# Counting edges on one core of a graph kernel: packed window register, one eviction per window, and both counting stretches of a block in a row

## The chip, the core and the metric

One core of one Trainium2 chip runs the whole kernel in one launch. The metric is device time in microseconds (us), the median of a few runs. A profiled execution gives the span of the program on the core and everything that the rows below show. TensorE is called PE, VectorE DVE, ScalarE ACT, GpSimd POOL and SyncE SP, as in the profile; PEld is PE's loading of weights, and a q behind a name (ACTq) is the engine's sequencer.

## What is computed

Four graph layers in a residual stack over 1250 nodes of 512 features and 20000 edges; the edges are sorted by `dst`. Two layers hold two convolutions each, so there are six:

```python
h = relu(layernorm(x)); x = x + relu(mean_in(h) @ W_l.T + b_l + h @ W_r.T)              # L0
h = relu(layernorm(x)); x = x + sage(relu(sage(h)))                                     # L1A, L1B
h = relu(layernorm(x)); x = x + layernorm(h + relu(h @ W_self.T + b + mean_out(h @ W_neigh.T + b_n)))  # L2
h = relu(layernorm(x)); x = x + gcn(relu(gcn(h)))                                       # L3A, L3B
```

`mean_in` and the sums in `sage` and `gcn` gather the rows of the sources of a node's edges (`segment_sum(x[src], dst)`), `mean_out` those of its targets.

## The kernel before

**Tiling.** The nodes are padded to 1280, ten tiles of 128 (`NT`). All six convolutions work with one dense matrix of edge counts between nodes: `count16` (targets on partitions) and its transpose `countT16`, integers of 16 bits. A sum over neighbours is then 20 matmuls of 128 x 512 per tile of nodes (`aggregate`, L1217), with the counts staged as floats by ACT (`stage`, L480, two buffers `cstage`) and the features as a high and a low part (`p_hi`, `p_lo`).

**Counting.** The matrix is built at the start of the program by one-hot matmuls. A block is one tile of 128 targets, a window is 64 of them, so a block has windows h = 0 and 1 and there are 20 windows. The sorted edges lie in tiles of 128. A table says for every window at which edge tile it begins and how many it touches, in groups of `RING` = 6 tiles. For this graph the windows take 6, 3, then eight times 2, then ten times 1 groups, 35 in all: blocks 1 to 4 have two groups in each window, blocks 5 to 9 one. For one group of six tiles DVE writes six one-hots of the source (`src_hot`, 128 x 640, `givers`, L717) and three of the receiver (`dst_hot`, L715), ACT the other three receivers (`receivers`: three Abs into `apart`, L446, and one Relu over all three, L450), and PE makes 12 matmuls of 320 columns (`count`, L1112). There is one ring of six slots, so DVE and ACT are at most one group ahead of PE. The sign of the receiver's number says to which half of 640 the source belongs, so a window's sums stand in PSUM as 64 targets of the lower half on partitions 0 to 63 and of the upper half on 64 to 127. ACT takes them out with two activations of 64 partitions x 640 (`counts_of`, L428), each with an accumulated sum for the degrees, and puts them straight into `count16` by target. SP transposes each block of `count16` by DMA (L288).

**Registers.** PE, DVE and ACT loop over the groups of a window with bounds from the table (L240, L1123). ACT and DVE load 12 registers for two blocks at a time at the top of their loops (6 at some ends), three for each window; PE loads two for a block.

**Order.** The counting is interleaved by hand with the dense work of the first convolution, L0: PE turns the features of block b (`turn`, L1133) and makes the two products of block b - 1, 12 matmuls of 512 columns each (`first_p`, `first_q`, L1140). In the loop PE does: count (b, 0), p of b - 1, count (b, 1), turn b, q of b - 1. ACT does: deviation of b, receivers (b, 0), eviction (b - 1, 1), receivers (b, 1), phi of b - 1, eviction (b, 0), hi of b. So an eviction stands behind the receivers of the window that follows. DVE does: givers (b, 0), own of b - 2, features of b, givers (b, 1), `p_lo` of b - 1, statistics of b + 1, lo of b. Each engine works strictly in its order; semaphores tie them: a matmul of a group waits for `first_rows` (the Relu of ACT) and `givers_ready` (DVE), a hot waits for `hot_used` (PE), the eviction for `counts_ready` (the last matmul of the window, L1118), `turn` for `z_ready` (DVE).

**After the counting** the six convolutions run one behind another, and PE has nearly no idle time in them.

## Time and profile before

| | us |
|---|---|
| median of 3 runs (722.85 to 723.21) | 723.08 |
| the profiled execution | 723.23 |
| its span | 721.5 |
| PE busy, whole span | 671.5 (93%) |
| DVE busy | 408.4 (57%) |
| ACT busy | 286.8 (40%) |

The chain of work that ended last goes by 81% over PE, 5% over issue, 5% DVE and 3% ACT. The engines' busy times overlap, so they don't add up to the span. PE is "busy" too when it runs at half its clock, which some stretches show.

### The profile page before, as it was taken

The page shows a single profiled execution, that of the slowest core. Times are in us where ns is not written, and L with a number is a line of the kernel's source. Part 1 is how long each engine was busy: PE and PEld are TensorE (multiplying, and loading weights), DVE is VectorE, ACT ScalarE, POOL GpSimd, SP SyncE. Part 2 cuts the span into 40 slices and gives each one's busy share as a digit, 9 for nine tenths or more (in the row PEclk, how much of TensorE's full clock was granted, in tenths as well). Part 3 has the DMA queues.
Part 4 walks back from the last instruction along what each step waited for, and adds up shares of the span by engine and source line. Part 5 has one row for each costly group of instructions (what it writes and reads, how often), then busy time and mean ns, then how long its engine had stood idle before and what let it go on. Part 6 is the DMA issues. An engine that isn't in the chain of part 4 may idle for free.

```text
span 721.5 us, 11380 instructions
## 1 busy us (share of the span) xinstructions
PE 671.5 (93%) x3199; PEld 526.2 (73%) x3200; DVE 408.4 (57%) x951; ACT 286.8 (40%) x525; POOL 18.3 (3%) x26
## 2 busy tenths in 40 slices
PE   4948888889899999999999999999999899999997
PEld 3325565666688888888888888888877678887786
DVE  6977776666357544332443466655799871247333
ACT  2656565576343222465212342212444352223321
POOL 2000000000000000000000000000322000000000
PEclk9979999999899999999999999999999999999999
DMA  7101211011402000210000210000200000000011
GB/s 248 48 1 25 72 31 22 18 36 36 106 0 73 1 0 0 76 58 1 0 0 0 75 58 1 0 0 1 75 0 1 0 2 1 0 1 0 31 59 55
DMA packets 22801, 21.94 MB, mean 30 GB/s; under 512 B 13676, under 2 KB 13988, under 8 KB 22760
## 3 DMA queue, kind: packets, MB, share of 16 engines
q1 hardware_dynamic: 21480, 18.85, 9.2%
q10 hardware_dynamic: 1280, 2.56, 1.0%
q8 instruction: 24, 0.39, 0.2%
q14 instruction: 17, 0.14, 0.1%
HBM read 15.57 MB, written 2.56 MB: 25 GB/s over the span
## 4 chain that ended last, share of the span: by engine, by line
PE 81%; issue 5%; DVE 5%; ACT 3%; ACTq 2%; DVEq 2%; DMA 1%; SPq 0%
PE ps L1217 35%; PE ps L1140 33%; PE ps L1112 8%; PE ps L1133 3%; ACTq L240 1%; DMA wstage<-in_L_gnn_W_l 1%; DVEq L240 1%; ACT cstage L480 1%; PE ps L1092 1%; DVE src_hot L717 1%; ACT count L428 1%; DVE own L948 1%; ACT apart L446 1%; PE ps L1080 0%; DVE stats L695 0%
## 5 line engine op out<-in xcount | busy, mean ns | idle before, releaser
L1217 PE MATMUL ps<-p_hi,cstage 128*128 128x512 f32 x600 | 236.2, 394 | 6.4 <-issue 4.6
L1217 PE MATMUL ps<-p_lo,cstage 128*128 128x512 f32 x600 | 235.0, 392 | 0.0
L1140 PE MATMUL ps<-w_hi,hT_hi 128*128 128x512 f32 x400 | 162.4, 406 | 2.1 <-DVE hT_lo L756 2.0
L1140 PE MATMUL ps<-w_hi,hT_lo 128*128 128x512 f32 x400 | 156.6, 391 | 0.0
L1140 PE MATMUL ps<-w_lo,hT_hi 128*128 128x512 f32 x400 | 156.0, 390 | 0.0
L1217 PEld LDWEIGHTS ps<-p_hi,cstage 128*128 128x128 f32 x600 | 113.6, 189 | 31.9 <-issue 8.4
L1217 PEld LDWEIGHTS ps<-p_lo,cstage 128*128 128x128 f32 x600 | 113.6, 189 | 23.3
L920 DVE SCALAR_TENSOR_TENSOR own<-ps,nodal,own 128x512 f32 (+1 forms) x60 | 44.9, 749 | 124.6 <-PE ps L1217 124.2
L480 ACT CAST cstage<-countT 128x1280 fp32r (+1 forms) x50 | 62.6, 1262 | 90.9 <-PE ps L1217 90.0
L1112 PE MATMUL ps<-src_hot,dst_hot 128*128 128x320 bf16 x420 | 76.2, 330 | 22.0 <-ACT dst_hot L450 14.4
L717 DVE TENSOR_SCALAR src_hot<-iota,nodeT 128x640 bf16<-128x640 f16 x210 | 74.5, 381 | 25.5 <-PE ps L1112 13.1
L1140 PEld LDWEIGHTS ps<-w_hi,hT_hi 128*128 128x128 f32 x400 | 75.3, 188 | 18.6 <-DVE hT_lo L756 1.8
L1140 PEld LDWEIGHTS ps<-w_hi,hT_lo 128*128 128x128 f32 x400 | 75.1, 188 | 16.7
L1140 PEld LDWEIGHTS ps<-w_lo,hT_hi 128*128 128x128 f32 x400 | 75.3, 188 | 13.9
L1112 PEld LDWEIGHTS ps<-src_hot,dst_hot 128*128 128x128 bf16 x420 | 38.6, 106 | 54.0 <-DVE src_hot L717 22.7
L467 ACT ACTIVATE hT_hi<-ps 128x512 fp32r<-128x512 f32 x60 | 35.7, 596 | 78.7 <-PE ps L1133 78.5
L763 DVE TENSOR_TENSOR p_lo<-ps,p_hi 128x512 f32 (+1 forms) x40 | 27.6, 691 | 64.2 <-ACT p_hi L473 64.0
L473 ACT ACTIVATE p_hi<-ps 128x512 f32 (+1 forms) x40 | 23.9, 598 | 77.5 <-PE ps L1140 77.4
L756 DVE SCALAR_TENSOR_TENSOR hT_lo<-ps,hT_hi 128x512 fp32r<-128x512 f32 x60 | 41.0, 684 | 5.7 <-ACT hT_hi L467 5.2
L437 ACT ACTIVATE nodal<-mv,eps (+1 forms) x40 | 11.8, 295 | 79.6 <-DVE mv L704 67.1
L1133 PE MATMUL ps<-ident,z 128*128 128x128 f32 x240 | 36.8, 276 | 4.6 <-DVE z L743 4.3
L1133 PEld LDWEIGHTS ps<-ident,z 128*128 128x128 f32 x240 | 28.9, 141 | 12.4 <-issue 5.4
(130 smaller groups left out, 477.8 us busy)
## 6 DMA issues: line engine op xcount, KB each, us to landing
x<-in_x ACTq DMA_DIRECT2D x1, 2304.0 KB
out_x<-x SPq DMA_DIRECT2D x9, 256.0 KB
wstage<-in_L_gnn_W SPq DMA_DIRECT2D x2, 1024.0 KB, 5.2
wstage<-in_L_gnn_W_l SPq DMA_DIRECT2D x1, 1024.0 KB, 8.8
w_own<-in_L_gnn_W_r SPq DMA_DIRECT2D x1, 1024.0 KB, 9.4
vec<-in_L_gnn_b SPq DMA_DIRECT2D x4, 256.0 KB, 5.5
wstage<-in_L_gnn_W1l SPq DMA_DIRECT2D x1, 1024.0 KB, 5.6
wstage<-in_L_gnn_W1r SPq DMA_DIRECT2D x1, 1024.0 KB, 5.4
```

The lines of the kernel that those rows point to most:

```text
L240: _, found = nc.values_load_multi_w_load_instructions(for_hots[0:1, bass.ds(2 * b, 2 * blocks), 0:3], engines=[engine.engine], bass_reorde ...
L467: nc.scalar.activation(hT_hi[:, r, :, :], ps[:, HT + r, :].rearrange("p (k n) -> p k n", k=KF), ACT.Relu).then_inc(hi_done, 1)
L473: nc.scalar.activation(p_hi[:, bass.ds(i, 1), :], ps[:, p_bank(s, r), :], ACT.Copy, scale=1.0 if CONVS[s]["own"] else dis[:, bass.ds(i, 1) ...
L480: nc.scalar.copy(cstage[:, r, :, :], columns(s, i)).then_inc(stage_ready, 1)
L717: nc.vector.tensor_scalar(src_hot[:, e, :], iota[:, :], nodeT[:, 1, bass.ds(t + e, 1)], None, ALU.is_equal).then_inc(givers_ready, 1)
L756: nc.vector.scalar_tensor_tensor(hT_lo[:, r, :, :], ps[:, HT + r, :].rearrange("p (k n) -> p k n", k=KF), 0.0, hT_hi[:, r, :, :].bitcast(F ...
L763: nc.vector.tensor_tensor(p_lo[:, bass.ds(i, 1), :], ps[:, p_bank(s, r), :], p_hi[:, bass.ds(i, 1), :].bitcast(F32), ALU.subtract).then_in ...
L920: nc.vector.scalar_tensor_tensor(own_, ps[:, AGG + r:AGG + r + 1, :], scale[:, bass.ds(i, 1)], own_, ALU.mult, ALU.add).then_inc(t_done, 1)
L1112: last = nc.tensor.matmul(ps[:, COUNT + 2 * h + k, 0:NS // 2], dst_hot[:, e, :], src_hot[:, e, k * (NS // 2):(k + 1) * (NS // 2)], start=F ...
L1133: last = nc.tensor.transpose(ps[:, HT + r, k * P:(k + 1) * P], z[:, r, k * P:(k + 1) * P], ident[:, :])
L1140: last = nc.tensor.matmul(ps[:, bank, :], a[:, r, k, :], w[:, slot, k, :], start=n == 0, stop=n == len(pairs) - 1)
L1217: last = nc.tensor.matmul(ps[:, AGG + r, :], cstage[:, part, k, :], p_[:, k, :], start=n == 1, stop=n == 2 * len(parts) * NT)
```

## The change

One register of the table per window holds both the first edge tile and the number of tiles (first tile in the low 8 bits). Every engine loads it once per window and keeps its own count of visited tiles. Eviction is one activation of 128 partitions x 640: `count16` now holds, for block b, the two source halves on the partitions and the two windows side by side. The transposing DMAs go by window, 20 instead of 10, and write a `countT16` in which the staging copies read 64 counts, then the other window's 64. For L2, which needs `count16` by target, two quarters are swapped through DRAM (`swap`) by four DMAs in SP's queue. ACT makes four of six receivers. PE does both counting stretches of a block, with the turning between them, and then both products. The steps of the table, the order of the first weights (W_l in two halves ahead of x) and the first two blocks are written anew.

```diff
-    HALF = RING // 2
+    BY_ACT = 4
-    def visits_of(engine, b, blocks):
-        _, found = nc.values_load_multi_w_load_instructions(
-            for_hots[0:1, bass.ds(2 * b, 2 * blocks), 0:3], engines=[engine.engine], bass_reorder=False)
...
+    def visits_of(engine, visited, b, h):
+        _, (packed,) = nc.values_load_multi_w_load_instructions(
+            tiles_of[0:1, window(b, h)], engines=[engine.engine], bass_reorder=False)
+        t0, length = engine.snap(packed & 255), engine.snap(packed >> 8)
+        n0 = engine.snap(visited, min_val=0, max_val=NW * (ETP + RING))
+        offset = engine.snap(t0 - n0)
...
+        engine.reg_mov(visited, n1)
+        return n0, n1, offset
 # SP
-            order = [("f", 0), ("v", rows[0]), ("f", 1), ("v", rows[1]), ("t", 0), ("t", 1), loads[0]]
+            order = [("f", 0), ("f", 1), ("f", 2), ("v", rows[0]), ("v", rows[1]), ("t", 0), ("t", 1), loads[0]]
...
+                    for h in range(2):
+                        sp.wait_ge(counts_out, 2 * what + h + 3)
+                        sp.dma_start_transpose(
+                            countT16[:, 2 * what + h, :, :].rearrange("p (c q) d -> p c (q d)", q=2),
+                            count16[:, what, h * NS:(h + 1) * NS]).then_inc(cT_loaded, 16)
 # ACT
-            act.wait_ge(src_loaded, 32 + 16 * bool(REST))
+            for k, loaded in enumerate((dst_loaded, src_loaded)):
+                act.wait_ge(loaded, 16 * (2 + bool(REST)))
+                nc.scalar.copy(e_f[:, k, :, :], e_int[:, k, :, :]).then_inc(cast_done, 1)
+            act.wait_ge(first_loaded[1], 16)
             act.wait_ge(x_pad_set, 1)
             dma_rows(act, x_dram, x, x_loaded)
...
-                for q in range(2):
-                    nc.scalar.activation(
-                        count16[WIN * h:WIN * h + WIN, bass.ds(b, 1), q * NS:(q + 1) * NS].rearrange(
-                            "p o (a n) -> p (o a) n", a=2),
...
+                nc.scalar.activation(count16[:, bass.ds(b, 1), h * NS:(h + 1) * NS].rearrange("p o (a n) -> p (o a) n", a=2),
+                                     ps[:, COUNT + 2 * h:COUNT + 2 * h + 2, 0:NS // 2], ACT.Copy,
+                                     accum_out=deg_win[:, bass.ds(b, 1), h]).then_inc(counts_out, 1)
...
+                deviation(0, b)
+                receivers(b, 0)
+                counts_of(b, 0)
+                receivers(b, 1)
+                hi(L0, b, r)
+                counts_of(b, 1)
+                phi(L0, b - 1, 1 - r)
 # DVE
+                givers(b, 0)
                 features(L0, b, r)
-                givers(b, 1, *second)
+                first_own(b - 2)
+                givers(b, 1)
+                lo(L0, b, r)
+                if not (isinstance(b, int) and b == NT - 1):
+                    statistics(0, b + 1)
                 p_rest(L0, b - 1, 1 - r)
 # PE
-                n1 = visits_end(b)
-                count(b, 0, n1[0])
+                count(b, 0)
+                turn(L0, b, r)
+                count(b, 1)
                 first_p(b - 1, 1 - r)
-                count(b, 1, n1[1])
-                turn(L0, b, r)
                 first_q(b - 1, 1 - r)
...
+            count(0, 0)
+            turn_first(1, (0, 1))
+            count(0, 1)
+            turn_first(1, (2, 3))
+            count(1, 0)
             pe.wait_ge(wlo_done, 2 * KF)
             turn(L0, 0, 0)
-            with pe.Fori(1, NT - 1, 2) as b0:
+            count(1, 1)
+            first_p(0, 0)
+            turn(L0, 1, 1)
+            first_q(0, 0)
+            with pe.Fori(2, NT - 1, 2) as b0:
```

ACT between the two windows of a block, in the loop, before: `apart` and `dst_hot` are the receivers (L442 to L450 their loop), `count_49` the eviction, here of the window (b - 1, 1), with the receivers of (b, 1) behind it.

```order
L450 ACTIVATE dst_hot<-apart 128x384 [waits hot_used]
L442 REGISTER_ALU
L442 COMPARE_AND_BRANCH
L426 REGISTER_ALU
L428 ISA [waits counts_ready]
L428 ACTIVATE count_49,deg_parts<-ps 64x640
L428 ISA
L428 ACTIVATE count_49,deg_parts<-ps 64x640
L442 UNCONDITIONAL_BRANCH
L442 ISA
L446 ISA [waits first_rows]
L446 ACTIVATE apart<-tab,nodeT 128x128
```

The same place after the change; the eviction is that of (b, 0), and L254 loads the window's register.

```order
L496 ACTIVATE dst_hot<-apart 128x512 [waits hot_used]
L486 REGISTER_ALU
L486 COMPARE_AND_BRANCH
L464 ISA [waits counts_ready]
L464 ACTIVATE count_49,deg_win<-ps 128x640
L254 REGISTER_ALU
L254 TENSOR_LOAD tiles_of
L257 ISA
L486 UNCONDITIONAL_BRANCH
L486 ISA
L491 ISA [waits first_rows]
L491 REGISTER_ALU
```

The rows read alike, but `counts_ready` is now the signal of the window whose receivers stand just ahead, so ACT comes to the receivers of (b, 1) only when PE is through with (b, 0).

PE behind the first counting stretch of a block, in the loop, before: L1118 ends the window, and the product p (L1140) follows.

```order
L1105 COMPARE_AND_BRANCH
L1118 MATMUL ps<-zeros 128x64
L1146 REGISTER_ALU
L1147 REGISTER_ALU [waits lo_done]
L1140 MATMUL ps<-w_hi,hT_hi 128x512 [waits plo_done]
```

And after, where the turning (L1173) and the start of the next window stand there.

```order
L1164 MATMUL ps<-zeros 128x64
L1169 REGISTER_ALU
L1171 REGISTER_ALU [waits z_ready]
L1173 MATMUL ps<-ident,z 128x128 [waits lo_done]
L1173 MATMUL ps<-ident,z 128x128 x3
L1148 REGISTER_ALU
L1150 MATMUL ps<-zeros 128x64 [waits counts_out]
L1150 MATMUL ps<-zeros 128x64
L254 ISA
L254 TENSOR_LOAD tiles_of
L257 ISA
L1152 UNCONDITIONAL_BRANCH
```

Twelve matmuls of 512 columns have moved from between the two windows to behind them, where 24 of them now stand in a row; four small ones are left between.

## Rows read from the trace of the kernel before

**Rows 1.** Windows by stage: start:end, length, busy PE PEld DVE ACT POOL, clock, DMA.
```profile
16.50:66.94 50.44, 37.99 (x220) 20.49 (x218) 39.76 (x134) 30.77 (x78) 0.00 (x0) 0.90 0.12 34
66.94:119.34 52.40, 44.55 (x246) 28.94 (x247) 42.14 (x143) 31.12 (x79) 0.00 (x0) 0.93 0.16 39
119.34:168.49 49.15, 43.64 (x233) 30.79 (x233) 32.01 (x102) 30.59 (x77) 0.00 (x0) 0.90 0.14 27
168.49:188.31 19.82, 15.60 (x82) 11.70 (x82) 9.71 (x29) 12.85 (x26) 0.00 (x0) 0.97 0.39 74
188.31:721.50 533.19, 523.58 (x2392) 429.56 (x2392) 274.20 (x504) 177.00 (x256) 13.35 (x10) 0.99 0.06 21
```

**Rows 2.** Register loads by line: count, min/median/max ns, first and last start.
```profile
L240 ACTq TENSOR_LOAD <-for_hots x6: 963/2652/2678, 11.8 to 165.0; - x6
L240 DVEq TENSOR_LOAD <-for_hots x5: 876/2793/2819, 11.8 to 155.6; - x5
...
L553 ACTq TENSOR_LOAD <-big_i x1: 294/294/294, 182.8 to 182.8; - x1
```

**Rows 3.** Timeline of PE: start, length, what, idle before it; counts of one window.
```profile
50.30 5.14 PE L1112 MATMUL ps<-src_hot,dst_hot 128*128 128x320 bf16 x24 [5.43 <-ACT dst_hot L450]
...
66.94 4.80 PE L1112 MATMUL ps<-src_hot,dst_hot 128*128 128x320 bf16 x24 [1.68 <-DVE src_hot L717]
...
84.68 5.02 PE L1112 MATMUL ps<-src_hot,dst_hot 128*128 128x320 bf16 x24 [2.73 <-ACT dst_hot L450]
...
92.45 3.59 PE L1112 MATMUL ps<-src_hot,dst_hot 128*128 128x320 bf16 x24
...
101.65 5.07 PE L1112 MATMUL ps<-src_hot,dst_hot 128*128 128x320 bf16 x24 [1.99 <-DVE src_hot L717]
```

**Rows 4.** Timeline of PE, blocks 7 to 9.
```profile
149.53 0.48 PE L1140 MATMUL ps<-w_hi,hT_hi 128*128 128x512 f32 x1
...
164.21 0.63 PE L1133 MATMUL ps<-ident,z 128*128 128x128 f32 x4
...
168.49 1.80 PE L1112 MATMUL ps<-src_hot,dst_hot 128*128 128x320 bf16 x12 [0.81 <-DVE src_hot L717]
...
170.12 0.19 PE L1118 MATMUL ps<-zeros 128*128 128x64 bf16 x1
```

**Rows 5.** Timeline of ACT: receivers, deviation, p_hi, eviction.
```profile
120.98 0.98 ACT L446 ACTIVATE apart<-tab,nodeT 128x128 bf16 x3
...
122.14 0.52 ACT L450 ACTIVATE dst_hot<-apart 128x384 bf16<-128x384 bf16 x1 [0.17 <-ACT apart L446]
...
144.31 0.29 ACT L437 ACTIVATE nodal<-mv,eps  x1 [2.77 <-issue]
...
152.64 0.60 ACT L473 ACTIVATE p_hi<-ps 128x512 f32 x1 [2.91 <-PE ps L1140]
...
170.36 0.70 ACT L428 ACTIVATE count<-ps 64x640 uint16<-64x640 f32 x1 [0.26 <-PE ps L1118]
...
171.29 0.70 ACT L428 ACTIVATE count<-ps 64x640 uint16<-64x640 f32 x1
```

**Rows 6.** Windows after two idles of PE, columns as in Rows 1.
```profile
66.00:71.70 5.70, 4.59 (x25) 1.62 (x25) 5.17 (x19) 3.82 (x11) 0.00 (x0) 1.00 0.02 4
85.00:87.50 2.50, 2.50 (x11) 1.43 (x10) 1.37 (x5) 1.60 (x5) 0.00 (x0) 0.50 0.00 0
```

**Rows 7.** Timeline of the start, all engines.
```profile
4.23 1.50 ACTq L255 DMA_DIRECT2D x<-in_x  x2
...
8.85 0.43 ACT L455 COPY nodeT<-ps 128x324 f32<-128x324 f32 x1 [5.95 <-PE ps L1052]
...
16.50 3.58 PE L1112 MATMUL ps<-src_hot,dst_hot 128*128 128x320 bf16 x24
```

**Rows 8.** DMA issues: a weight load without the load of x beside it.
```profile
wstage<-in_L_gnn_W SPq DMA_DIRECT2D x2, 1024.0 KB, 5.2
```

**Rows 9.** Costliest groups: ACT's staging copies.
```profile
L480 ACT CAST cstage<-countT 128x1280 fp32r (+1 forms) x50 | 62.6, 1262 | 90.9 <-PE ps L1217 90.0
```

More of the change, by code:

```diff
@@ L113, in gnn_kernel @@
     dst_hot, _ = place("dst_hot", [P, RING, P], BF16, place.end)
-    apart, _ = place("apart", [P, HALF, P], BF16, place.end)
     assert place.end <= cstage_at + 2 * NT * P * 4
@@ L142, in gnn_kernel @@
     length, _ = place("length", [P, 1], F32, place.end)
-    span, _ = place("span", [P, 3], F32, place.end)
-    before, _ = place("before", [P, NW + 1], F32, place.end)
-    starts, _ = place("starts", [1, 32], F32, place.end)
+    base, _ = place("base", [P, 1], F32, place.end)
+    span, _ = place("span", [P, 1], F32, place.end)
     assert place.end <= own_at + 5 * D * 4
     deg_parts, _ = place("deg_parts", [P, 2, NT], F32, exact_at)
+    deg_win, _ = place("deg_win", [P, NT, 2], F32, place.end)
     assert at[0] <= nc.sbuf_usable_end, (at[0], nc.sbuf_usable_end)
     ps = nc.alloc_psum_tensor("ps", [P, 8, 512], F32)
+    swap = nc.dram_tensor("swap", (2, WIN, NT, NS), U16, kind="Internal").ap()
     HT, PP, QQ, AGG = 0, 2, 4, 6
@@ L438, in deviation, with receivers @@
                                      bias=eps[:, 0:1]).then_inc(std_done, 1)
-            def receivers(b, h, t0, t1, shift):
-                with act.Fori(t0, t1, RING) as t:
-                    act.wait_ge(first_rows, t + shift + RING)
-                    for e in range(HALF):
-                        nc.scalar.activation(apart[:, e:e + 1, :], tab[:, window(b, h), :], ACT.Abs, scale=-1.0,
-                                             bias=nodeT[:, 0, bass.ds(t + e, 1)]).then_inc(apart_done, 2)
-                    act.wait_ge(apart_done, t + shift + RING)
-                    act.wait_ge(hot_used, t + shift + HALF)
-                    nc.scalar.activation(dst_hot[:, 0:HALF, :], apart[:, :, :], ACT.Relu, scale=-1.0,
+            visited = act.alloc_register("act_visited")
+            act.reg_mov(visited, 0)
+            def receivers(b, h):
+                n0, n1, offset = visits_of(act, visited, b, h)
+                with act.Fori(n0, n1, RING) as n:
+                    t = tile_at(act, n, offset)
+                    act.wait_ge(first_rows, n + RING)
+                    for e in range(BY_ACT):
+                        last = nc.scalar.activation(apart[:, e:e + 1, :], tab[:, window(b, h), :], ACT.Abs, scale=-1.0,
+                                                    bias=nodeT[:, 0, bass.ds(t + e, 1)])
+                    last.then_inc(apart_done, RING)
+                    act.wait_ge(apart_done, n + RING)
+                    act.wait_ge(hot_used, n + BY_ACT)
+                    nc.scalar.activation(dst_hot[:, 0:BY_ACT, :], apart[:, :, :], ACT.Relu, scale=-1.0,
                                          bias=1.0).then_inc(first_rows, RING)
@@ L824, in _, with merged @@
-            merged_end(1, 1)
+            givers(1, 0)
+            split_first(1, range(2, KF))
+            features(L0, 1, 1)
+            givers(1, 1)
+            statistics(0, 2)
+            lo(L0, 0, 0)
+            p_rest(L0, 0, 0)
+            lo(L0, 1, 1)
+            dve.wait_ge(vec_loaded[VSLOT[L0]], VCOUNT[L0])
+            def merged(b, r):
+                givers(b, 0)
+                features(L0, b, r)
+                first_own(b - 2)
[3 more added lines that the diff above has]
+                    statistics(0, b + 1)
+                p_rest(L0, b - 1, 1 - r)
```

293 lines of the change are left out of this document (143 added, 150 removed).

## The prediction

> **What bounds the kernel now.** I read the windows by stage first [rows 1]. From 188.3 us to the end PE is busy for 523.6 of 533.2 us, and the change puts nothing new on PE there. The room is in the front: PE is busy 38.0 of 50.4 us up to 66.94, 44.6 of 52.4 in the three blocks 2 to 4, 43.6 of 49.2 in blocks 5 to 8, 15.6 of 19.8 in block 9 and the bridge. That is 30 us of idle, and the clock stands at 0.90 to 0.97, so part of the busy time is at 1.2 instead of 2.4 GHz.
>
> Then the register loads [rows 2]: 2.65 us on ACT and 2.79 on DVE for 12 registers, four or five times each. They alternate, and behind each of them PE waits: 2.73 us for ACT's `dst_hot` at 84.68, 1.99 for DVE's `src_hot` at 101.65, 5.43 at 50.30 [rows 3]. Behind such a wait 24 matmuls take 5.0 us, against 3.6 without one, and the clock is 0.50 there [rows 3, 6]. A wait of 1.68 us at 66.94 left the clock at 1.00 [rows 3, 6]. So a stall of 2 us or more cost some 1.5 us over its own length.
>
> **The loads and the eviction.** A load of one register took 0.294 us [rows 2], so I take 0.3. It starts while the instruction before it runs, as the loads of before do. With 0.2 to 0.3 us of register work behind it, it hides under an eviction (0.9), a `p_lo` (0.7) or a deviation with p_hi (0.9) nearly whole. The eviction: the two of a window start 0.93 us apart [rows 5], half remains, and 128 partitions I price as 64, since 640 columns are what a lane does. ACT saves 0.9 us per window, 18 us in all, but ACT is not full (30.6 of 49.2 us), so this counts only where ACT is waited for. The Trainium skill, "DMA: Bandwidth & Descriptors", section Latency and other measured facts, gives a floor of about 600 ns for a `tensor_load`, whatever its size; that speaks against 20 small loads. The row for one register is half of that floor, so the trace does not agree; by the floor a window would pay up to 0.3 us more and the sum below would be up to 5 us higher.
>
> **The new order, block with one group per window.** s is the first count matmul of (b, 0).
> - PE needs 1.63 us from the first matmul to L1118 [rows 4].
> - ACT now evicts (b, 0) before it makes the receivers of (b, 1). From L1118 to the eviction 0.24 (170.12 to 170.36), 0.93 to the next instruction [rows 4, 5]. Three Abs and the wait took 1.16 (120.98 to 122.14); a fourth makes 1.46, at 0.30 each. The Relu of 512 columns 0.60, as p_hi has for 512 (0.52 for 384) [rows 5]. 0.14 to the matmul. Sum 3.37 us from the end of (b, 0) to the start of (b, 1). Only the turning, 0.63 [rows 4], lies in it: 2.7 us of idle PE in every block. Before, one product of 2.8 us and receivers already made lay there.
> - DVE is in time: features, own and six hots end about 3.6 us after L1118, and PE reaches the sixth hot later.
> - Count (b, 1) 1.68. Then both products, 5.7 us. p ends after 2.8; p_hi starts 3.11 behind the first product matmul (149.53 to 152.64 [rows 4, 5]), takes 0.60, deviation 0.29, then 1.46 + 0.60 + 0.14 for the receivers of the next block: 6.20. PE waits 0.5 again. DVE starts its hots about 1 us behind the start of `p_lo` and is not later.
> - Block: 1.63 + 3.37 + 1.68 + 6.20 = 12.9 us. Four of them 51.5, against 49.15 in the trace [rows 1]: **+2.4**. These four of before hold two loads and their slow clock and average 12.3; the two without a load take about 11.
>
> **Two groups per window** (blocks 2 to 4). ACT needs after a Relu 0.13, then 1.46 + 0.60 + 0.12 = 2.3 us for the next four receivers, PE is through with a group in 1.7, so each second group costs 1.7 + 0.5. DVE's 2.35 us per group (before 2.5, one hot of 0.16 less) trails from PE's first slot and is no later. Block: 12.9 + 2 x 2.2 = 17.25; three of them 51.7 against 52.4: **-0.7**.
>
> **Block 9.** The middle gap of 2.7 replaces one of about 0.9 (0.81 at 168.49 is of that kind [rows 4]): **+1.8**. The bridge to the aggregation (registers, branch) keeps its order behind q.
>
> **The start.** The table loses six short steps on DVE, W_l is ahead of x. W_l alone lands in 5.2 us [rows 8] from an issue near 3.3, in shorter pieces, so 8.5 to 9.5, say 9.2. But ACT waits for that before it issues x (1.50), then node table (0.43), two weight copies (1.0), load (0.3), receivers (2.2) [rows 5, 7]: first count at 14.6 against 16.50, a lead of 1.9. Windows 0 and 1 have nine groups, at 0.16 each: lead 3.0. At count (1, 0) the load of 2.65 us on ACT and half of the weight splits no longer lie ahead of it: I get 42.6 against 50.30, a lead of 7.7. In block 1 it is partly lost: splits and features stand between the givers on DVE, hots are not made ahead, p(0) waits for lo behind two more pieces of statistics, and hi(1), q(0), lo(1), and the next givers follow in a chain. Step by step I reach count (2, 0) at 63.9 against 66.94: **-3.0**. Bounds: the whole lead kept, -7.7, to all of it lost, 0.
>
> **The clock.** The new middle gap (2.7 us idle, with turning in it) is between the 1.68 that kept the clock and the 2.73 that lost it. There are eight such gaps. Below: none loses the clock, 0; above: all, 8 x 1.5 = 12. The nearest row is 1.99, which lost it; but turning breaks the gap up. I take three: **+4.5**. The two new idles of 0.5 us stay below 1.68.
>
> **Hidden parts.** The staging copies read runs of 64 counts instead of 128. 1262 ns for 1280 counts is the price of a count, not of a run, and 90 us of idle lie ahead of them [rows 9]: 0; twice the price is the bound above, where only the first of a convolution shows. The swap and the 20 transposes are SP's and DMA's; SP waited for ACT's counts before, and the last transposes have some 8 us of products ahead of the first use. PE's own loads lie under its queued matmuls. Four small copies for the degrees lie beside p(9).
>
> **Sum.** 723.23 (the profiled execution, 721.5 of span and 1.7 around it; 0.15 above the median of the runs) - 3.0 - 0.7 + 2.4 + 1.8 + 4.5 = **728.2 us**, 0.7% slower.
>
> **Rivals.**
> - *The clock holds.* No middle gap loses it. Then 723.7, no change. For: idle of 1.7 us is left behind the turning on the side of (b, 1) at some phases, and 1.68 did no harm. Against: 1.99 did.
> - *The start carries it (faster).* Place: count (1, 0) to count (2, 0). If DVE's chain in block 1 is shorter than I set it, the 7.7 us of lead stay, and with one lost clock the time is 723.2 - 7.7 - 0.7 + 2.4 + 1.8 + 1.5 = 720.5. It decides from a start of count (2, 0) before about 59.5 with three lost clocks. For: loads of 2.7 us are gone on both engines. Against: block 1 is bound by DVE's order, not by loads.
> - *The clock is lost nearly everywhere.* Blocks with two groups last near the same time, so what one shows the others may too. Seven: +6 more, 734.
> - *Copies or loads dear.* Staging copies at twice their price, six first pairs: about 5 to 8 more, 735.
> - *The change doesn't do what it says*, so that a load of one register costs as 12 do: 2.7 us per window would stand on ACT's path, over 740. The row of 0.294 speaks against it.
>
> **How the numbers follow.** Forecast (2 to 5 lost clocks) 0.42, its own range 725 to 731; clock holds 0.15; start carries 0.22; clock lost everywhere 0.14; copies 0.05; loads 0.02. About 0.2% or 1.4 us is what a measurement tells from no change. The faster case is below 721.6 nearly whole; of "clock holds" 0.03 is faster, 0.09 the same, 0.03 slower, and of the forecast a little is the same. Faster 0.24, same 0.12, slower 0.64. The range from 718 to 735 leaves out the ends of the second and third rival and the last.
>
> **What the profile after would show.** Loads of L254 near 0.3 us; evictions 20 of 128 x 640 at 0.7; in each block PE idle some 2.7 us ahead of count (b, 1), released by ACT's `dst_hot`, and 0.5 ahead of count (b + 1, 0); blocks of 12.9 and 17.2 us, longer by 1.5 where the clock is 0.50; first count near 14.6, count (2, 0) near 64; from the first aggregation on the same 533 us. I am wrong if PE waits there for DVE and not for ACT, if the middle gap is below 2 us, or if the front ends earlier than before.

## The result, and the profile after

| | before | after |
|---|---|---|
| median, us | 723.0 | 729.76 |
| lowest and highest | 722.85 to 723.21 | 726.27 to 731.05 |
| ratio, 95% interval | | 1.0079 [1.0044, 1.0115] |
| the profiled execution, its span | 723.23, 721.5 | 726.27, 724.5 |
| PE busy, mean granted clock | 671.5, 0.975 | 664.1, 0.988 |

The kernel became 0.8% slower. The forecast was 728.2 us in a range from 718 to 735. The profiled execution of the changed kernel happens to be the fastest of the four; the other three took 729.6 to 731.1 us, and their granted clock over the whole program is lower, 0.984 to 0.986 against 0.988. So the profile shows a little less than what the median has.

The windows by stage of the changed kernel, cut at the same places of the program as [rows 1] (first count, count (2, 0), count (5, 0), count (9, 0), first matmul of the aggregation), with the same columns:

```profile
13.83:61.22 47.39, 36.15 (x216) 21.72 (x217) 39.00 (x127) 32.41 (x85) 0.00 (x0) 0.93 0.24 74
61.22:116.66 55.44, 42.04 (x247) 29.69 (x247) 37.24 (x122) 31.54 (x81) 0.00 (x0) 0.97 0.16 37
116.66:171.69 55.03, 40.67 (x233) 30.60 (x233) 31.75 (x98) 26.77 (x68) 0.00 (x0) 0.97 0.12 24
171.69:192.15 20.46, 15.33 (x82) 11.93 (x82) 9.61 (x33) 9.15 (x18) 0.00 (x0) 1.00 0.23 56
192.15:724.50 532.35, 522.62 (x2392) 428.98 (x2392) 275.39 (x506) 177.85 (x258) 13.37 (x10) 1.00 0.09 28
```

Against [rows 1]: the start up to count (2, 0) ends at 61.22 instead of 66.94, 5.72 us earlier. Blocks 2 to 4 take 55.44 instead of 52.40, blocks 5 to 8 take 55.03 instead of 49.15, block 9 with the bridge 20.46 instead of 19.82, and the rest 532.35 instead of 533.19. The sum is +3.0 us, the difference of the spans. PE is busy less everywhere, in better clock; it waits more.

The register loads of the changed kernel, by line (count, minimum, median and maximum in ns), to be held against [rows 2]:

```profile
L254 PEldq TENSOR_LOAD <-tiles_of x20: 298/304/623, 10.5 to 173.0; - x20
L254 ACTq TENSOR_LOAD <-tiles_of x20: 273/278/492, 10.6 to 173.9; - x20
L254 DVEq TENSOR_LOAD <-tiles_of x20: 301/305/556, 10.6 to 172.2; - x20
```

A load of one word takes 0.28 to 0.31 us (medians of three engines), instead of 2.65 to 2.79 us for twelve. The Trainium skill, "DMA: Bandwidth & Descriptors", section Latency and other measured facts, gives about 600 ns as the floor of a `tensor_load`; the medians of the 60 loads here are half of that, so the trace does not agree. Near it came only single ones: the first load of each engine (492 to 556 ns) and one of PE's at 35.4 us, the 623 ns of its row.

The timeline of PE in the changed kernel: counts of one group (x12) or of two (x24, where the records ran together), with the idle time before them in brackets, to be held against [rows 3, 4, 7]:

```profile
13.83 1.80 PE L1159 MATMUL ps<-src_hot,dst_hot 128*128 128x320 bf16 x12 [1.70 <-ACT dst_hot L496]
...
41.42 5.78 PE L1159 MATMUL ps<-src_hot,dst_hot 128*128 128x320 bf16 x24 [4.90 <-ACT dst_hot L496]
...
61.22 1.80 PE L1159 MATMUL ps<-src_hot,dst_hot 128*128 128x320 bf16 x12 [0.82 <-DVE src_hot L762]
...
79.17 1.80 PE L1159 MATMUL ps<-src_hot,dst_hot 128*128 128x320 bf16 x12 [0.63 <-ACT dst_hot L496]
...
86.94 5.11 PE L1159 MATMUL ps<-src_hot,dst_hot 128*128 128x320 bf16 x24 [3.04 <-ACT dst_hot L496]
...
121.88 3.19 PE L1159 MATMUL ps<-src_hot,dst_hot 128*128 128x320 bf16 x12 [2.86 <-ACT dst_hot L496]
...
136.82 1.80 PE L1159 MATMUL ps<-src_hot,dst_hot 128*128 128x320 bf16 x12 [2.66 <-ACT dst_hot L496]
...
171.69 1.80 PE L1159 MATMUL ps<-src_hot,dst_hot 128*128 128x320 bf16 x12 [0.62 <-DVE src_hot L762]
...
176.89 1.80 PE L1159 MATMUL ps<-src_hot,dst_hot 128*128 128x320 bf16 x12 [2.85 <-ACT dst_hot L496]
```

The counts of a window (b, 1) wait 2.6 to 3.0 us (the middle wait from here on), in all eight blocks of the loop, and each time for ACT's `dst_hot`; the counts of a window (b, 0) wait 0.6 to 1.0. Behind two of the eight middle waits, at 86.94 and 121.88, the matmuls are slow: 12 take 3.19 instead of 1.80 us, and the granted clock from 121.9 to 125.0 is 0.54, near the lower of its two levels (1.2 of 2.4 GHz). Such a drop is called a lost clock below. The timeline of PE and ACT in the changed kernel at one such wait, in block 9, to be held against [rows 5]:

```profile
173.32 0.19 PE L1164 MATMUL ps<-zeros 128*128 128x64 bf16 x1
...
173.67 0.70 ACT L464 ACTIVATE count<-ps 128x640 f32 x1 [2.11 <-PE ps L1164]
...
174.27 0.19 ACT L464 ACTIVATION_READ_ACCUMULATOR count<-ps  x1
...
174.68 1.28 ACT L491 ACTIVATE apart<-tab,nodeT 128x128 bf16 x4 [0.22 <-issue]
...
176.13 0.63 ACT L496 ACTIVATE dst_hot<-apart 128x512 bf16<-128x512 bf16 x1 [0.17 <-ACT apart L491]
```

This is the path that the prediction drew: last matmul of (9, 0) at L1164, eviction 0.35 us later, its accumulator read, four Abs (L491), one Relu (L496), and the count at 176.89, 3.57 us behind L1164. The start of the changed kernel, and its staging copies, against [rows 7, 9]:

```profile
8.15 1.38 ACTq L276 DMA_DIRECT2D x<-in_x  x2
...
10.06 0.43 ACT L501 COPY nodeT<-ps 128x324 f32<-128x324 f32 x1 [5.60 <-issue]
...
L529 ACT CAST cstage<-countT 128x1280 fp32r (+1 forms) x50 | 62.7, 1263 | 88.8 <-PE ps L1259 88.0
```

ACT issues x at 8.15 instead of 4.23, since it waits for W_l's first half, and yet the first count stands at 13.83 instead of 16.50. The staging copies cost 1263 ns, as before.

### The profile page after: what moved, and what is told of

It reads as the page before. It is cut to its first block, busy times and chain, and to the rows that moved or that the text cites. A ratio compares the mean times of both kernels' runs of the same rounds, so it can differ in the third digit from the quotient of the medians.

```text
span 724.5 us, 11458 instructions
## 1 busy us (share of the span) xinstructions
PE 664.1 (92%) x3199; PEld 528.3 (73%) x3200; DVE 401.5 (55%) x911; ACT 283.4 (39%) x522; POOL 18.1 (2%) x25
## 4 chain that ended last, share of the span: by engine, by line
PE 79%; issue 6%; ACT 6%; DVE 5%; ACTq 2%; DVEq 1%; DMA 1%; SPq 0%
PE ps L1259 35%; PE ps L1180 33%; PE ps L1159 8%; PE ps L1173 3%; ACT apart L491 2%; ACT dst_hot L496 2%; DVE src_hot L762 1%; ACT cstage L529 1%; DVE own L994 1%; DMA wstage<-in_L_gnn_W_l 1%; ACTq L254 1%; ACT p_hi L520 1%; DVE stats L735 1%; PE ps L1121 0%; ACTq L491 0%
## 5 line engine op out<-in xcount | busy, mean ns | idle before, releaser
L1159 PE MATMUL ps<-src_hot,dst_hot 128*128 128x320 bf16 x420 | 69.6, 317 | 42.3 <-ACT dst_hot L496 34.4
L529 ACT CAST cstage<-countT 128x1280 fp32r (+1 forms) x50 | 62.7, 1263 | 88.8 <-PE ps L1259 88.0
L1180 PEld LDWEIGHTS ps<-w_hi,hT_lo 128*128 128x128 f32 x400 | 75.1, 188 | 16.3
L762 DVE TENSOR_SCALAR src_hot<-iota,nodeT 128x640 bf16<-128x640 f16 x210 | 71.5, 381 | 13.9 <-PE ps L1159 7.2
L491 ACT ACTIVATE apart<-tab,nodeT 128x128 bf16 (+1 forms) x140 | 44.7, 391 | 8.7 <-issue 4.5
L1173 PE MATMUL ps<-ident,z 128*128 128x128 f32 x240 | 36.4, 274 | 0.2 <-DVE z L788 0.2
```

The lines of the kernel that those rows point to most:

```text
L491: last = nc.scalar.activation(apart[:, e:e + 1, :], tab[:, window(b, h), :], ACT.Abs, scale=-1.0, bias=nodeT[:, 0, bass.ds(t + e, 1)])
L529: nc.scalar.copy(stage_of(s, r), columns(s, i)).then_inc(stage_ready, 1)
L762: nc.vector.tensor_scalar(src_hot[:, e, 0:NS], iota[:, :], nodeT[:, 1, bass.ds(t + e, 1)], None, ALU.is_equal).then_inc(givers_ready, 1)
L1159: last = nc.tensor.matmul(ps[:, COUNT + 2 * h + k, 0:NS // 2], dst_hot[:, e, :], src_hot[:, e, k * (NS // 2):(k + 1) * (NS // 2)], start=F ...
L1173: last = nc.tensor.transpose(ps[:, HT + r, k * P:(k + 1) * P], z[:, r, k * P:(k + 1) * P], ident[:, :])
L1180: last = nc.tensor.matmul(ps[:, bank, :], a[:, r, k, :], w[:, slot, k, :], start=n == 0, stop=n == len(pairs) - 1)
```

## The experiments

Twelve kernels ran. The packed register is read unbounded in the changed kernel; in all experiments its upper part is masked, which puts two short sequencer instructions more into each window on each of three engines (the trace of the first has 120 more in all, for 20 windows). PE's program holds eight windows, four ahead of the loop and four in it, so it grows by 16. So the first experiment is the changed kernel with that mask alone, and those behind it are held against it.

**The mask.**

```diff
-        t0, length = engine.snap(packed & 255), engine.snap(packed >> 8)
+        t0, length = engine.snap(packed & 255), engine.snap((packed >> 8) & 255)
```

> The changed kernel with one more register operation per window (the number of tiles is masked to 8 bits); the other experiments stand on it and it is their base. Every theory: the same time as the changed kernel, 726 to 731 us, with the spread between runs made by how many of the eight middle gaps lose the clock.

Measured: 734.7 us (734.4 to 736.0), ratio to before 1.0158 [1.0139, 1.0177], 4.9 us more than the changed kernel. That was not expected. Between the two profiled executions it is 8.1 us: 2.7 up to count (2, 0), 2.1 in the blocks, where three clocks are lost instead of two, and 3.3 from the aggregation on. Four rows of PE from it:

```profile
90.53 5.14 PE L1159 MATMUL ps<-src_hot,dst_hot 128*128 128x320 bf16 x24 [2.86 <-ACT dst_hot L496]
...
110.00 1.80 PE L1159 MATMUL ps<-src_hot,dst_hot 128*128 128x320 bf16 x12 [2.86 <-ACT dst_hot L496]
...
196.92 0.47 PE L1259 MATMUL ps<-p_hi,cstage 128*128 128x512 f32 x1 [2.28 <-issue]
...
199.58 0.80 PE L1259 MATMUL ps<-p_lo,cstage 128*128 128x512 f32 x1 [2.19 <-issue]
```

The first two show counts behind the same idle of 2.86 us, the one at half speed, the other (its first group) at full speed. The last two show where the largest part lies: behind the first matmul of the aggregation PE waits 2.19 us more before the second, where the changed kernel and the kernel before have no wait. A matter of where instructions lie in the program would look like this, so it was tried.

**The mask, with 48 matmuls of 64 zero columns ahead of the first count.**

```diff
+                if isinstance(b, int) and (b, h) == (0, 0):
+                    for k in range(48):
+                        nc.tensor.matmul(ps[:, COUNT + 2 * h + (k & 1), 0:64], zeros[:, :], zeros[:, 0:64], start=True, stop=True)
```

> The changed kernel with the masked register, and 48 matmuls of 64 zero columns ahead of the first counting matmul, where PE is idle anyway for some 2 us. They do no work; they move the rest of PE's program by as many instructions as the filled gap did. To be held against the masked kernel (734.7 us), whose trace shows a second wait of 2.19 us, named issue, between the first two matmuls of the aggregation, and a slow clock twice as long behind it; the changed kernel and the one with the filled gap show none. If that wait is a matter of where PE's instructions lie in the program, it goes: -2.2 for the wait and -1.1 for the clock, 731 to 732 us, near the changed kernel's 729.8. Rival: the wait comes from the loads and masks or from the timing of other engines; then it stays and the time is 734 to 736.

Measured: 730.78 us (728.3 to 731.5), 3.9 less than with the mask alone. The first two matmuls of the aggregation there:

```profile
197.37 0.76 PE L1263 MATMUL ps<-p_hi,cstage 128*128 128x512 f32 x1 [2.90 <-issue]
...
197.94 0.63 PE L1263 MATMUL ps<-p_lo,cstage 128*128 128x512 f32 x1
```

The second wait is gone. From the first of these matmuls to the end of the span it takes 532.3 us, and 535.7 with the mask alone: 3.4 us for the wait and the clock behind it. The start gives 2.0 more: the first matmuls of the count take 300 ns instead of 474, and count (2, 0) stands at 61.91 instead of 63.87. All three kernels with these 48 matmuls have a fast first count, but so have two without them (the changed one and the one with two evictions in the order of before), so this part may be chance. The blocks between took 135.5 instead of 133.1 us in this profile, because four clocks were lost and not three. What is left for the mask itself is the 1.0 us between the medians of this kernel and the changed one, less than the spread of either. The Trainium skill, "Runtime: NRT & Kernel Launch", section Instruction fetch mechanics, says that an engine's program is refilled in blocks of 256 instructions. The rows fit it (16 instructions more ahead of the place came with the wait, 96 more took it away), but they do not show the fetch itself, so the mechanism of this wait stays open.

**ACT's order: the receivers of (b, 1) ahead of the eviction of (b, 0).**

```diff
                 receivers(b, 0)
+                receivers(b, 1)
                 counts_of(b, 0)
-                receivers(b, 1)
                 hi(L0, b, r)
```

> ACT alone gets another order in the loop: receivers (b,0), receivers (b,1), then the evictions (b,0) and (b,1); PE, DVE and all else as changed. My theory (the eviction of (b,0) ahead of the receivers of (b,1) makes the 2.7 us gap in every block): the receivers of (b,1) are ready some 0.7 us after L1164, the gap falls to under 1 us, count (b,1) ends when DVE's six hots are made, about 2.5 us after L1164 instead of 5.2. That is 2.7 us in each of eight blocks, and no clock is lost: about 703 us (699 to 707), faster than both kernels. Rival (two counting stretches in a row are the trouble by themselves, since the ring holds one group and DVE cannot make the hots ahead): PE then waits for DVE in the same place nearly as long, and the time stays above 722 us.

Measured: 713.29 us (712.1 to 713.6), 21.4 less than with the mask. ACT and PE between the windows of block 6:

```profile
136.57 0.19 PE L1164 MATMUL ps<-zeros 128*128 128x64 bf16 x1
...
136.74 0.63 ACT L496 ACTIVATE dst_hot<-apart 128x512 bf16<-128x512 bf16 x1 [0.17 <-PE ps L1159]
...
137.27 0.69 ACT L464 ACTIVATE count<-ps 128x640 f32 x1
...
137.50 2.21 PE L1159 MATMUL ps<-src_hot,dst_hot 128*128 128x320 bf16 x12 [0.21 <-DVE src_hot L762]
```

Relu of (6, 1) at 136.74 while PE is at its last matmul of (6, 0), eviction behind it, and the count waits 0.21 us. One line moved on ACT is worth 21 us: eight waits of 2.86 that become 0.2 to 0.4, and three lost clocks that are kept. The forecast of 699 to 707 was still missed. The masked kernel's own 4.9 us are in the time, and the rival is true in a small part: the matmuls of (b, 1) now wait singly for DVE's hots, 12 of them taking 2.2 us instead of 1.80 in the blocks with one group.

**The order of before on PE, ACT and DVE in the loops, with packed register, one eviction and the new start.**

```diff
 # PE
                 count(b, 0)
-                turn(L0, b, r)
+                first_p(b - 1, 1 - r)
                 count(b, 1)
-                first_p(b - 1, 1 - r)
+                turn(L0, b, r)
                 first_q(b - 1, 1 - r)
...
 # ACT
                 receivers(b, 0)
+                counts_of(b - 1, 1)
+                receivers(b, 1)
+                phi(L0, b - 1, 1 - r)
                 counts_of(b, 0)
-                receivers(b, 1)
                 hi(L0, b, r)
-                counts_of(b, 1)
-                phi(L0, b - 1, 1 - r)
...
```

> From block 2 on PE, ACT and DVE get the order of the kernel before (count, p, count, turn, q; the eviction of (b,0) and hi behind phi; the eviction of (b,1) in the next block), with the packed register, the single eviction and four receivers on ACT kept. My theory: loads are short and no gap over 1.1 us is left, so one-group blocks take about 11 us (13.4 in the changed kernel) and two-group blocks about 15.5 (18), with block 9 some 2 us shorter: 704 to 709 us. Rival (it is not the order but ACT's fourth receiver, or the loads that now stand in every window, that cost): 720 us or more.

Measured: 707.02 us (706.1 to 708.1), ratio to before 0.977 [0.975, 0.9789]. Its windows by stage, cut as above:

```profile
14.06:62.85 48.79, 37.73 (x217) 22.06 (x217) 39.71 (x128) 31.86 (x83) 0.00 (x0) 0.93 0.22 68
62.85:108.19 45.34, 39.86 (x246) 28.43 (x247) 37.02 (x123) 30.98 (x82) 0.00 (x0) 1.00 0.18 46
108.19:151.75 43.56, 38.84 (x233) 29.20 (x233) 31.75 (x97) 26.60 (x69) 0.00 (x0) 1.00 0.15 30
151.75:169.58 17.83, 15.20 (x81) 11.71 (x82) 9.97 (x32) 9.93 (x21) 0.00 (x0) 1.00 0.26 73
```

Blocks 2 to 4 take 45.34, 5 to 8 take 43.56 us, 7.1 and 5.6 less than before the change [rows 1], and the clock is 1.00 in all of them. So the parts of the change other than the order in the loops are worth 16.6 us (against the 723.6 of the kernel before in the same series), and the order costs 27.7: 21.4 by the one line on ACT, 6.3 by PE's order, DVE's and the rest of ACT's, which were not told apart. By stages the 16.3 us between the profiles are 4.1 in the start, 14.6 in the blocks and bridge, less 2.4 for the extra wait at the aggregation, which this kernel has too.

**Three receivers by ACT instead of four** (`BY_ACT = 3`).

> The changed kernel with the masked register, with one number different: ACT makes three of six receivers and DVE three, as before the change. To be held against the masked kernel (734.7 us). My theory is that the idle PE between the two windows of a block is ACT's path of eviction, four Abs and one Relu. One Abs less is 0.30 us and a Relu over 384 instead of 512 columns 0.08, so each middle gap falls from 2.86 to about 2.48, eight times: -3.0, and each second group of a window loses 0.2 to 0.4 us of its 0.57 idle, six pairs: up to -2. One or two of the three lost clocks may be kept: -1.5. I expect 729 to 732. Rival: DVE, with one more hot of 0.16 us per group, is what the gap waits for as soon as ACT is shorter; then the time stays at 734 to 736, and the gap is released by DVE's src_hot.

Measured: 734.36 us (732.9 to 734.9): the same as with the mask. Four rows of PE:

```profile
70.81 1.80 PE L1159 MATMUL ps<-src_hot,dst_hot 128*128 128x320 bf16 x12 [1.83 <-DVE src_hot L762]
...
102.11 2.23 PE L1159 MATMUL ps<-src_hot,dst_hot 128*128 128x320 bf16 x12 [0.17 <-ACT dst_hot L496]
...
107.36 1.80 PE L1159 MATMUL ps<-src_hot,dst_hot 128*128 128x320 bf16 x12 [1.82 <-DVE src_hot L762]
...
136.63 3.21 PE L1159 MATMUL ps<-src_hot,dst_hot 128*128 128x320 bf16 x12 [1.81 <-DVE src_hot L762]
```

The middle wait fell: to 1.8 (once 2.3) in the four blocks where DVE sets it now, and to 2.2 to 2.5 in the four where it is ACT's. In other groups the matmuls wait singly for DVE's hots (12 take 2.23 us at 102.11). The clock was lost behind five of the eight middle waits, against three with the mask; at 136.63 it was lost behind 1.81 us of idle, and at 107.36 it held behind 1.82. So the forecast of 729 to 732 missed: what the shorter steps gave, DVE's waits and the lost clocks took. The rival had the time right, and the releaser in half of the blocks.

**The wait filled with 24 zero matmuls of 128 columns.**

```diff
+                if h == 1 and not isinstance(b, int):
+                    for k in range(24):
+                        nc.tensor.matmul(ps[:, COUNT + 2 * h + (k & 1), 0:P], zeros[:, :], zeros[:, :], start=True, stop=True)
```

> As changed, but ahead of count (b,1) of blocks 2 to 9 PE makes 24 matmuls of 128 columns of zeros into the count bank, which is zeroed again behind them (about 1.4 us, inside the gap of 2.7 us). They add nothing to the result. If lost clocks cost 1.5 us each and come from the idle of the gap, none of the eight gaps loses the clock: about 724 us, and the runs lie within 1 us of one another. Rival (the spread and the slow stretches come from elsewhere): mean and spread as for the changed kernel. If the zeros are in the way of the count, 2 us or more are added instead.

Measured: 726.73 us (725.8 to 727.1, eight runs), 8.0 less than with the mask. Two middle waits:

```profile
88.44 1.80 PE L1163 MATMUL ps<-src_hot,dst_hot 128*128 128x320 bf16 x12 [1.53 <-ACT dst_hot L496]
...
177.06 1.80 PE L1163 MATMUL ps<-src_hot,dst_hot 128*128 128x320 bf16 x12 [1.52 <-ACT dst_hot L496]
```

The counts stand no earlier (5.22 us from count (9, 0) to count (9, 1), as with the mask), but no middle wait loses the clock. The granted clock over the whole program is 0.992 to 0.995 in all eight executions, and 0.981 to 0.986 in the five with the mask. The zero matmuls and their weight loads also moved PE's program, and the second wait is away: 532.7 us from the first matmul of the aggregation, 3.0 of the 8.0. Another 1.3 lie in the start. From count (2, 0) to the aggregation it took 129.7 instead of 133.1 us: three lost clocks that are kept, 1.1 us each.

**The eviction as two activations of 64 partitions**, in the changed order and in the order of before:

```diff
-                nc.scalar.activation(count16[:, ...], ps[:, ...], ACT.Copy, accum_out=deg_win[:, ...]).then_inc(counts_out, 1)
+                for w in range(2):
+                    last = nc.scalar.activation(count16[WIN * w:WIN * w + WIN, ...], ps[WIN * w:WIN * w + WIN, ...], ...)
+                last.then_inc(counts_out, 1)
```

> The changed kernel with the masked register, and the eviction of a window made again by two activations of 64 partitions x 640, one behind another (the layout is the new one, only the instruction is split). To be held against the masked kernel (734.7 us). ACT's path theory: the second activation, 0.93 us behind the first, stands on the path from the end of window (b, 0) to the receivers of (b, 1), so each of the eight middle gaps grows from 2.86 to 3.8: +7.4 us, and more gaps lose the clock, up to five more at 1.3: 742 to 749 us. Rival: the gap is bound by something else (DVE's givers, or registers), and the time stays within 1 us of 734.7.

> The kernel with the packed register and the order of before in the loops (707.0 us), with the eviction of a window made by two activations of 64 partitions x 640. In this order an eviction stands behind the receivers of the window that follows and has a product of 2.8 us of PE beside it. If the eviction's length counts only where PE waits for it, the time stays at 706.5 to 708. Rival: ACT as a whole bounds these blocks, and each window pays 0.93 us: 16 windows in the loops, +15, about 722.

Measured: 753.89 us (752.0 to 754.6) in the changed order, 19.2 more than with the mask; 709.01 (706.7 to 710.4) in the order of before, 2.0 more, with ranges that overlap. In the changed order, the count of (4, 1), then the evictions of (8, 0) and the count of (8, 1):

```profile
114.70 1.80 PE L1163 MATMUL ps<-src_hot,dst_hot 128*128 128x320 bf16 x12 [3.58 <-ACT dst_hot L500]
...
175.00 0.70 ACT L465 ACTIVATE count<-ps 64x640 f32 x1 [2.12 <-PE ps L1168]
...
175.80 0.70 ACT L465 ACTIVATE count<-ps 64x640 f32 x1
...
178.94 3.38 PE L1163 MATMUL ps<-src_hot,dst_hot 128*128 128x320 bf16 x12 [3.58 <-ACT dst_hot L500]
```

The second activation starts 0.80 us behind the first, PE waits 3.58 instead of 2.86, and six of eight middle waits lose the clock. A block with one group takes 14.5 us where the clock held and 15.8 to 17.1 where it did not. I had set 742 to 749; the lost clocks were dearer, up to 2.6 us, than the 1.3 I gave them, a further one was lost behind count (2, 0), and that count stands 1.1 us later. The same instruction costs 19 us in one place, lost clocks included, and about 2 in the other.

**A load of twelve words again, for the first window of each pair of blocks, in the order of before.**

```diff
-        _, (packed,) = nc.values_load_multi_w_load_instructions(
-            tiles_of[0:1, window(b, h)], engines=[engine.engine], bass_reorder=False)
+        one = tiles_of[0:1, window(b, h)]
+        _, (packed, *unused) = nc.values_load_multi_w_load_instructions(
+            one.to_broadcast([1, 12]) if wide else one, engines=[engine.engine], bass_reorder=False)
...
-                receivers(b, 0)
+                receivers(b, 0, r == 0)
...
-                givers(b, 0)
+                givers(b, 0, r == 0)
```

> The kernel with the packed register and the order of before in the loops (707.0 us), where ACT and DVE, for the first window of each pair of blocks, read twelve registers at once (twelve times the same word, one of them used) in place of one. Four pairs. A load of twelve took 2.7 us before, one takes 0.3. In the loop ACT comes from its last piece of block b - 1 to the load and then to the receivers, for which PE already waits 0.9 to 1.2 us, so 2.4 us come on top four times, 9.6, and the clock is lost behind each, 1.5 x 4 = 6: 717 to 723 us. That would make the loads the cause of most of the 16 us between the kernel before and this order. Rival: the long load lies beside the products of PE, as a sequencer's work that nobody waits for: 707 to 710. If the width of a load did not matter at all, 707.

Measured: 719.98 us (ten of its twelve runs 717.4 to 722.1, the others 724.8 and, unexplained, 1340.8), 13.0 more than without. The load, and the counts behind it:

```profile
L255 ACTq TENSOR_LOAD <-tiles_of x20: 272/280/2602, 10.5 to 163.6; - x20
...
65.69 1.80 PE L1160 MATMUL ps<-src_hot,dst_hot 128*128 128x320 bf16 x12 [2.97 <-ACT dst_hot L497]
...
98.17 5.07 PE L1160 MATMUL ps<-src_hot,dst_hot 128*128 128x320 bf16 x24 [3.28 <-ACT dst_hot L497]
...
127.32 1.80 PE L1160 MATMUL ps<-src_hot,dst_hot 128*128 128x320 bf16 x12 [3.48 <-ACT dst_hot L497]
```

Twelve words took 2.60 us on ACT (the maximum in its row), and PE waits 3.0 to 3.5 us where it waited 0.7 to 1.2. So long loads cost 13 us in this order, most of the 14.6 that the blocks and bridge had gained. Behind 2.97 and 3.48 us of idle the clock held; behind 3.28 it did not, and in the fourth place, behind 3.49, it fell after the first count matmuls.

**The zero matmuls in the kernel with the order of before.**

> The same 48 zero matmuls in the kernel with the packed register and the order of before in the loops (707.0 us), whose trace shows 2.18 us of the same wait. If it goes: 703 to 704 us. If the place where the instructions lie is not the cause, 707 to 708.

Measured: 702.08 us (701.7 to 702.7), 4.9 less than 707.02. The second wait is gone there as well (531.8 instead of 535.6 us from the first matmul of the aggregation), and the first count is fast again (count (2, 0) at 61.79 instead of 62.85).

**Block 1 begun earlier** (order of before in the loops):

```diff
 # ACT
             deviation(0, 0)
-            deviation(0, 1)
             receivers(1, 0)
...
             receivers(1, 1)
+            hi(L0, 0, 0)
             counts_of(1, 0)
-            hi(L0, 0, 0)
+            deviation(0, 1)
             phi(L0, 0, 0)
...
 # DVE
             statistics(0, 0)
+            givers(1, 0)
             split_first(1, range(0, 2))
+            features(L0, 0, 0)
+            split_first(1, range(2, KF))
+            givers(1, 1)
+            lo(L0, 0, 0)
             statistics(0, 1)
-            features(L0, 0, 0)
-            givers(1, 0)
-            split_first(1, range(2, KF))
             features(L0, 1, 1)
-            givers(1, 1)
             statistics(0, 2)
-            lo(L0, 0, 0)
             p_rest(L0, 0, 0)
```

> The kernel with the packed register and the order of before in the loops (707.0 us), with the hots and receivers of window (1, 0) made before the second tile's statistics and deviation, those of (1, 1) before the second tile's features, and the eviction (0, 1) behind the receivers. There count (1, 0) waits 5.02 us for ACT's receivers, which stand behind the deviation of tile 1. DVE is busy in block 1 nearly without a break, so of the 5 us I expect 2 to 3 back, and the clock that is lost behind the idle (1.2): count (2, 0) at 59.5 to 61 instead of 62.85, and 703.5 to 705.5 us. Rival, as in the prediction: block 1 is bound by DVE's chain whatever the order, and what count (1, 0) gains is waited for ahead of the turning of tile 0 or of p(0): 706.5 to 708.

Measured: 703.81 us (703.3 to 704.1), 3.2 less than 707.02. PE in block 1 and at count (2, 0):

```profile
40.96 1.80 PE L1159 MATMUL ps<-src_hot,dst_hot 128*128 128x320 bf16 x12 [2.70 <-DVE src_hot L762]
...
46.96 0.66 PE L1173 MATMUL ps<-ident,z 128*128 128x128 f32 x4 [1.87 <-DVE w_lo L724]
...
58.79 1.80 PE L1159 MATMUL ps<-src_hot,dst_hot 128*128 128x320 bf16 x12 [0.71 <-ACT dst_hot L496]
```

Count (1, 0) waits 2.70 instead of 5.02 us, and count (2, 0) stands at 58.79 instead of 62.85, 4.1 us earlier. Now the turning of tile 0 waits, 1.87 us for the last weight split: part of the rival is true, but most of the gain stays.

**Both together.**

> The version the runs point to: packed register, one eviction, the order of before in the loops, block 1 begun earlier, and the 48 zero matmuls ahead of the first count. Block 1 begun earlier gave count (2, 0) 4.1 us earlier (58.79 against 62.85) although the clock was lost at the first count, and the zero matmuls took away the second wait at the aggregation. If the two are independent: 702.1 - 4.1 = 698 us, between 697 and 699. Rival: the gain of the one is the gain of the other, through the clock at the start; then 700 to 702.

Measured: 698.89 us (698.1 to 700.2), ratio to before 0.9648 [0.9627, 0.9669]. The two gains add up, within the 697 to 699 that were expected. It is the fastest of all, 3.5% below the kernel before and 31 us below the changed one.

## Why the prediction was right

The sum came within 2 us of both: 728.2 against 726.27 in the profiled execution and 729.76 in the median. The mechanism that it named, ACT's eviction ahead of the receivers, is the one that the runs show. That the number came so near is in part luck: its terms did not all hold, and their errors went both ways. The measured terms below are those of the profiled execution.

- *Loads and eviction.* Right: 0.28 to 0.31 us against 0.3, and one eviction of 0.70. That the saved eviction counts only where ACT is waited for was the right rule: 19 us on the path, about 2 off it.
- *The middle gap.* The cause is right and shown: eight waits behind `dst_hot`, and they go when ACT's order is turned round. Size 3.57 from L1164 against 3.37: the eviction starts 0.35 and not 0.24 behind it, and the next instruction 1.01 and not 0.93 behind that.
- *Blocks with one group.* 13.2 to 13.7 without a lost clock, against 12.9: the middle gap is 0.2 longer, and the wait ahead of count (b + 1, 0) is 0.6 to 1.0 and not 0.5. Four of them, less the one lost clock of some 1.6, come to +4.3 instead of +2.4.
- *Blocks with two groups.* 17.9 against 17.25: the same two waits, and the second group starts 2.37 us behind the first and not 2.2. Here the prediction didn't use its own sum, which gave 2.3 for ACT's next receivers. Three of them without the clock are +1.4 instead of -0.7. This is the term that failed in sign, by 2.1 us.
- *The start.* -5.7 instead of -3.0. The first count came at 13.83, not 14.6, and count (1, 0) at 41.42, not 42.6. From there to count (2, 0) it took 19.8 us, not 21.3: I had made DVE's chain in block 1 too long. (The lead of 3.0 behind nine groups at 0.16 should read 3.3 by its own terms.) The reordered block 1 shows that order holds some of it: another 4.1 us could be had.
- *Block 9.* The middle gap grew by 2.0, near the 1.8 of the prediction (2.85 against 0.88), but the wait of the bridge shrank from 3.33 to 2.29: +0.6 instead of +1.8. That the bridge keeps its wait was the mistake. Why it shrank stays open: over the experiments it is 2.28 to 2.90; in the changed order it is 2.28 with the mask alone, and with 96 instructions more it is 2.30 in one kernel and 2.90 in the other. The count of (9, 1) before, and the bridge before and after:

```profile
174.09 1.80 PE L1112 MATMUL ps<-src_hot,dst_hot 128*128 128x320 bf16 x12 [0.88 <-ACT dst_hot L450]
188.31 0.77 PE L1217 MATMUL ps<-p_hi,cstage 128*128 128x512 f32 x1 [3.33 <-issue]
192.15 0.47 PE L1259 MATMUL ps<-p_hi,cstage 128*128 128x512 f32 x1 [2.29 <-issue]
```

- *From the aggregation on.* Set at no change; it took 0.8 us less, of which the faster matmuls behind the bridge (0.47 and 0.77 us in the rows above) are a part.
- *The clock.* Three lost, 1.5 us each, was the guess. The profiled execution lost two in the middle gaps, 1.4 to 1.9 us each (blocks of 19.57 against 17.9, 15.05 against 13.2 to 13.7). The masked kernel lost three, and with the zero matmuls ahead four. That the slower executions of the changed kernel lost more is likely: their recorded clock is 0.984 to 0.986 against 0.988, and the masked kernel's is 0.981 in the two executions of 735.8 and 736.0 us and 0.986 in the three of 734.4 to 734.7. Two more executions of the changed kernel are on record, 725.74 us at 0.988 and 729.83 at 0.982. No profile of a slower one is there, and one (731.05 at 0.986) does not fit the order of the clocks.

So the blocks of the loop were set 4.0 us too cheap (1.9 and 2.1), and the start 2.7, block 9 1.2, the clock 1.2 and the rest 0.8 too dear; together that is the 1.9 us by which the forecast lies above the profiled execution. Of the rivals, "the start carries it" was half true (of 8.9 us of lead at count (1, 0), 5.7 stayed; its sign, count (2, 0) before 59.5, did not come) and was eaten by the blocks. "Clock holds" and "clock lost everywhere" did not come: two, three and four of eight were lost in the three profiled kernels with this gap. Copies and loads were not dear.

## What to carry to other kernels

When an instruction is moved on a strict engine, ask what the next engine waits for behind it: an eviction that can wait belongs behind the work that another engine needs next, and here this one line outweighed every real saving. A shorter instruction is worth what it is on the path, so price the same saving in the old order too; the best version keeps the new parts and the old order. Change one thing per run: a gain of 16.6 us and a loss of 27.7 in one edit came out as the masked kernel's 1.6%.

## What the runs showed of the hardware that was not expected

- The same idle time loses the clock or not. In one execution 2.86 us of idle left PE at half clock at 90.53 and at full clock at 110.00. Over all runs the longest middle wait that kept it was 3.58 us and the shortest that lost it 1.81, while one of 1.82 in the same execution kept it, so my bound between 1.68 and 1.99 was none. The Trainium skill, "TensorE: Matmul & The Clock Gate", part 1, says that the monitor of activity runs freely beside the kernel, so that the moment of the change varies from run to run; the rows fit that, but show no monitor.
- The bridge between two loops can hold an extra wait of 1.7 to 2.6 us, named issue, between two matmuls that wait for nothing else. It was in the masked kernel and in the seven variants that left PE's number of instructions as it was, and in none of the four with 96 more. With the clock behind it, it is worth 3.0 to 3.8 us. That a shift of the program takes it away is shown; why is not.
- Zero matmuls in a wait cost no time (the counts behind them stand as far from the window before as without), and in the profiled execution no middle wait of 1.5 us that they left lost the clock. The eight executions lie within 1.3 us; the five with the mask alone lie within 1.6, so the spread alone shows little, but the recorded clock is higher in all eight.
